# First rows in two loads ahead of U3, and 11 warming transposes in place of 13

## The chip, the cores and the metric
One core of a Trainium2 chip runs the program. The metric is the device time of one execution in microseconds (us), the median of several runs.

## What is computed
A gated graph network over x (64 batches, 128 nodes, 256 features, float32), three steps with one dense adjacency, then a residual and a layer norm:

```python
h = x
for _ in range(3):
    a_in = jnp.einsum('nm,bmd->bnd', adj, h)
    a_out = jnp.einsum('nm,bmd->bnd', adj, h)
    av = jnp.concatenate([a_in, a_out], axis=-1)
    z = sigmoid(av @ w3.T + w3_b + h @ u3.T + u3_b)
    r = sigmoid(av @ w4.T + w4_b + h @ u3.T + u3_b)
    hv = tanh(av @ w5.T + w5_b + (r * h) @ u5.T + u5_b)
    h = (1 - z) * h + z * hv
out = layernorm(x + h)
```

Both aggregates use the same adjacency, so the kernel adds the two halves of w3, w4 and w5 and has one aggregate.

## The kernel before, in words
**Tiling.** The 64 batches are worked on in groups of 4 batches (512 rows); 4 groups make a round, and there are 4 rounds. Within a round each group has three steps, so a round has 12 frames (group and step), interleaved so that TensorE always has a product of one frame to do while the other engines work on another. State is held features first (hT, xT: two chunks of 128 features by 512 rows) for the dense products, and nodes first (hn, x_in) for the aggregate. Every float32 operand of a steady product is split into a high part (ScalarE casts it to fp32r) and a low part (VectorE subtracts), and a product is three matmuls: high weight with low state, low with high, high with high (lines 416 to 420).

**Order.** Each engine has its instruction stream written out by hand and waits on semaphores. SP issues nearly all DMAs; ScalarE issues the first two and the stores. VectorE splits, transposes blocks and updates the state, ScalarE evaluates sigmoid and tanh and makes high parts. GpSimd makes the identity (line 1142) and small constants.

**The start**, which the change touches, has its own code.
- ScalarE issues two loads: `first_in` (line 747), which per partition (node) holds the rows of the first 4 batches (4 x 256 floats) and the transposed adjacency (128 floats), 576 KB; then `lead_in` (line 748), which holds U3 and half 0 of the first group's state, features first, 512 KB. Behind these it loads the activation table (line 751), splits the two halves of the state (line 680), the first aggregate (line 656), W4 and W5 (line 745).
- SP waits for a constant of GpSimd (line 375), then issues half 1 of that state (line 376, 256 KB), W4 (512 KB, line 377 through 373), the biases, W5, W3, the rows of the second group (line 381), and further loads.
- VectorE waits for `lead_in` (line 991), splits U3 (992, 994), makes the low part of state half 0 (line 918), sums the two halves of W4 (line 977), then the low part of state half 1, the low parts of the aggregate (line 865), the low part of W4 (987), the biases (1004), and the sums of W5 and W3.
- TensorE waits for the identity and does 13 transposes of it into a bank that is overwritten later (`keep_warm`, lines 546 to 549), then the first aggregate in full float32 (`first_aggregate`, lines 430 to 441; 2 halves of 2 batches, each batch 2 chunks, 8 matmuls), then the parts of U3 (`first_u`), of W4, of W5 and of W3 (`first_dense`). The aggregate waits for `rows_first` (line 432), the parts of U3 for the splits.

Of the kernel before, what the change touches and what calls it, by code (L numbers as in the profile page):

```python
# [54 lines left out]
P = 128  # L55
EPS = 1e-5


def build(nc, x_rows, first_rows, second_rows, lead, x_cols, w3_t, w4_t, w5_t, u5_t, biases, out_rows):
    N, B, D = out_rows.shape  # L60
    ROWS = 512
    GB = ROWS // N
    C = D // P
    HB = GB // 2
# [7 lines left out]
    DMA = 16  # L72
# [7 lines left out]
    with ctx:  # L80
        def sb(name, shape, dt=F32):
            return ctx.enter_context(nc.sbuf_tensor(name, shape, dt))
# [4 lines left out]
        def sem(name):  # L87
            return ctx.enter_context(nc.semaphore(name))
# [10 lines left out]
        bias = sb("bias", [P, 3, C])  # L99
        wt_hi = [sb(f"wt_hi{k}", [P, C, D], F32R) for k in range(5)]  # L100
        wt_lo = [sb(f"wt_lo{k}", [P, C, D], F32R) for k in range(5)]
        first_in = sb("first_in", [P, GB * D + N])
        adjT = first_in[:, GB * D:GB * D + N]
        W3, W4, W5, U3, U5 = range(5)
        BZ, BR, BV = range(3)

# [16 lines left out]
        aT = sb("aT", [P, QUADS, LINE])  # L123
        z = [sb(f"z{k}", [P, C, ROWS]) for k in range(2)]
        y = [sb(f"y{k}", [P, GB, D]) for k in range(2)]
        x_first = [first_in[:, 0:GB * D].rearrange("p (b d) -> p b d", b=GB), y[1]]
        y_tail = sb("y_tail", [P, GB, D])


# [24 lines left out]
        def by_chunk(bank):  # L154

            return bank.rearrange("p (c r) -> p c r", c=C)
# [24 lines left out]


        x_loaded = [sem(f"x_loaded{k}") for k in range(2)]
        rows_first = sem("rows_first")
        stored = [sem(f"stored{k}") for k in range(2)]


# [15 lines left out]
        rows_second = sem("rows_second")  # L203
# [95 lines left out]
        def _(sp):  # L299
            def load_cols(i, q):  # L300
                sp.dma_start(xT[q][:, :, :], x_cols[bass.ds(SLOTS * i + q, 1), :, :, :]
                             .rearrange("g p c r -> p (g c) r")).then_inc(xT_loaded[q], DMA)
# [69 lines left out]
            def load_wide(k):  # L372
                sp.dma_start(wide[k][:, :, :, :], wide_in[k]).then_inc(w_loaded[k], DMA)
# [4 lines left out]
            sp.dma_start(bias_in[:, :, :], biases).then_inc(bias_loaded, DMA)  # L378
            load_wide(W5)
            load_wide(W3)  # L380
            sp.dma_start(x_first[1][:, :, :], second_rows).then_inc(rows_second, DMA)
            load_cols(0, 1)
            sp.dma_start(square[1][:, :, :], u5_t).then_inc(w_loaded[U5], DMA)
            load_rows(0, 2)
# [30 lines left out]
        def _(pe):  # L415
# [13 lines left out]

            def first_aggregate(j):  # L430

                pe.wait_ge(rows_second if j == 1 else rows_first, DMA)
                for hf in range(2):
                    bank = by_chunk(ps_a[:, hf, :])
                    for bb in range(HB):
                        b = hf * HB + bb
                        for c in range(C):
                            done = nc.tensor.matmul(bank[:, c, bb * N:(bb + 1) * N],  # L438
                                                    x_first[j][:, b, c * P:(c + 1) * P],
                                                    adjT[:, :], start=True, stop=True)  # L440
                    done.then_inc(a_ready, 1)

# [21 lines left out]
            def update_product(i, j, carry):  # L464

                if carry or j >= 2:
                    pe.wait_ge(z_ready, C * frames(*two_before(i, j)))
                u_product(i, j)
# [21 lines left out]
            def second_half(i, j, carry):  # L490

                gate_r(i, j)
                value(i, j, carry)
                if j < FR - 1:
                    gate_z(i, j)

            def candidate(i, j):

                pe.wait_ge(rh_hi_ready, C * frames(i, j))
                pe.wait_ge(rh_lo_ready, C * frames(i, j))  # L500
                for oc in range(C):
                    dense(ps_v, U5, oc, rh_hi, rh_lo, False, True).then_inc(vpre_ready, 1)

            def weight_ready(k):
                pe.wait_ge(wt_hi_ready, PREPARED.index(k) + 1)
                pe.wait_ge(wt_lo_ready, PREPARED.index(k) + 1)
# [6 lines left out]
            def first_u():  # L513

                pe.wait_ge(u3_hi_ready, 1)
                for kc in range(C):
                    pe.wait_ge(hT_hi_ready, kc + 1)
                    for oc in range(C):
                        part(ps_g[0], wt_hi, U3, oc, kc, hT_hi, kc == 0, False)
                    pe.wait_ge(u3_lo_ready, 1)  # L520
                    for oc in range(C):
                        part(ps_g[0], wt_lo, U3, oc, kc, hT_hi, False, False)
                for kc in range(C):
                    pe.wait_ge(hT_lo_ready, kc + 1)
                    for oc in range(C):
                        part(ps_g[0], wt_hi, U3, oc, kc, hT_lo, False, False)

            def first_dense(dst, k, start, stop, done):

                pe.wait_ge(wt_hi_ready, PREPARED.index(k) + 1)  # L530
                pe.wait_ge(a_hi_ready, 2)
                for kc in range(C):
                    for oc in range(C):
                        part(dst, wt_hi, k, oc, kc, aT_hi, start and kc == 0, False)
                pe.wait_ge(a_lo_ready, 2)
                for kc in range(C):
                    for oc in range(C):
                        part(dst, wt_hi, k, oc, kc, aT_lo, False, False)
                pe.wait_ge(wt_lo_ready, PREPARED.index(k) + 1)
                for oc in range(C):  # L540
                    for kc in range(C):
                        end = part(dst, wt_lo, k, oc, kc, aT_hi, False, stop and kc == C - 1)
                    if done:
                        end.then_inc(done, 1)

            def keep_warm(n):

                for _ in range(n):
                    nc.tensor.transpose(ps_g[0][:, 0, 0:P], ident[:, :], ident[:, :])  # L549

            def first_round():

                pe.wait_ge(ident_ready, 1)
                keep_warm(13)
                first_aggregate(0)
                first_u()
                first_dense(ps_g[0], W4, False, True, rpre_ready)
                first_dense(ps_v, W5, True, False, None)
                pe.wait_ge(r_ready, C)
                first_dense(ps_g[0], W3, False, True, zpre_ready)  # L560
                first_aggregate(1)
                update_product(0, 1, False)
                weight_ready(U5)
                candidate(0, 0)
                aggregate(0, 2, first=True)
                for j in range(1, FR - 2):
                    frame(0, j, False)
                second_half(0, FR - 2, False)
# [84 lines left out]
        def _(act):  # L653
# [91 lines left out]
                nc.scalar.copy(wt_hi[k][:, :, :], weight(k)[:, :, :]).then_inc(wt_hi_ready, 1)  # L745

            act.dma_start(first_in[:, :], first_rows).then_inc(rows_first, DMA)
            act.dma_start(lead_in[:, 0:C * D + ROWS], lead).then_inc(lead_loaded, DMA)

            act.wait_ge(neg_half_ready, 1)  # L750
# [19 lines left out]
            j = FR - 1  # L770
# [432 lines left out]
```

## Time and profile before

| | us |
|---|---|
| median of 3 runs | 735.11 (735.06 to 735.43) |
| the profiled execution | 734.97 |
| its span, first to last instruction | 732.9 |
| TensorE busy (page, engines) | 726.1 |
| VectorE busy | 635.7 |
| ScalarE busy | 419.4 |

The span is the time between the first and the last instruction that the profile shows; the profiled execution's own time is 2.1 us more. PE is TensorE's matmuls, PEld its weight loads, which run beside the matmuls, DVE is VectorE, ACT ScalarE, SP SyncE. ACTq and SPq are instructions that issue a DMA. Records of the matmuls overlap, since they are pipelined, so the distance between starts says more than the length of one. A name with an arrow is what is written and what it is written from. In the views by DMA queue q1 is SP's queue and q10 is ScalarE's.

### The profile page before, as it was taken

To read this page: it belongs to the slowest core of one execution; us is meant where nothing else is said; L and a number is where in the kernel's file an instruction comes from. 1 tells how busy PE (TensorE), PEld (TensorE's weight loads), DVE (VectorE), ACT (ScalarE), POOL (GpSimd) and SP (SyncE) were. 2 spreads that over 40 slices of the span, in tenths; PEclk is the share of its full clock that TensorE was granted. 3 is DMA by queue.
4 is the path that set the end of the run, shared out by engine and by line. 5 is a ranking of instruction groups with operands and counts; after the bars stand their busy time and mean duration, and the time that the engine had idled before them with its cause. 6 is when DMAs were issued, how large, how long until landed. Compare 5 with 4: busy or idle time off the path is not lost.

```text
span 732.9 us, 9687 instructions
## 1 busy us (share of the span) xinstructions
PE 726.1 (99%) x3237; PEld 602.3 (82%) x3237; DVE 635.7 (87%) x932; ACT 419.4 (57%) x647; POOL 29.9 (4%) x71
## 2 busy tenths in 40 slices
PE   9999999999999999999999999999999999999997
PEld 7888888888888888888888888888888888888886
DVE  6788898889998888898999888899899987899887
ACT  5645655465666654565566754565556664565546
POOL 0000000000010000000011000000011000000013
PEclk9999999999999999999999999999999999999999
DMA  8145454446766445445567445544467544544442
GB/s 345 61 145 168 136 184 143 140 148 186 237 225 194 160 148 172 152 137 167 188 237 229 156 139 172 184 140 134 163 203 254 195 159 143 164 132 134 142 145 116
DMA packets 74183, 124.13 MB, mean 169 GB/s; under 512 B 8368, under 2 KB 55472, under 8 KB 74160
## 3 DMA queue, kind: packets, MB, share of 16 engines
q1 hardware_dynamic: 72144, 116.43, 48.8%
q10 hardware_dynamic: 2016, 7.41, 2.8%
q8 instruction: 13, 0.21, 0.1%
q14 instruction: 10, 0.08, 0.0%
HBM read 67.18 MB, written 56.62 MB: 169 GB/s over the span
## 4 chain that ended last, share of the span: by engine, by line
PE 98%; DVE 1%; ACT 0%; issue 0%; POOLq 0%; POOL 0%; DVEq 0%
PE ps_g L420 17%; PE ps_g L418 17%; PE ps_g L419 17%; PE ps_v L420 12%; PE ps_v L418 12%; PE ps_v L419 12%; PE ps_a L420 3%; PE ps_a L418 3%; PE ps_a L419 3%; PE ps_g L510 1%; PE ps_a L438 1%; PE ps_g L549 0%; PE ps_v L510 0%; DVE dz L1072 0%; DVE stats L1037 0%
## 5 line engine op out<-in xcount | busy, mean ns | idle before, releaser
L685 ACT ACTIVATE ps_v<-ps_v,bias 128x512 f32<-128x512 f32 x94 | 62.2, 662 | 182.7 <-PE ps_v L420 182.7
L418 PE MATMUL ps_g<-aT_hi,wt_lo 128*128 128x512 f32 (+1 forms) x380 | 147.1, 387 | 0.0
L420 PE MATMUL ps_g<-aT_hi,wt_hi 128*128 128x512 f32 (+1 forms) x380 | 147.0, 387 | 0.0
L419 PE MATMUL ps_g<-aT_lo,wt_hi 128*128 128x512 f32 (+1 forms) x380 | 147.0, 387 | 0.0
L724 ACT ACTIVATE z<-ps_g,bias 128x512 f32<-128x512 f32 x94 | 64.8, 690 | 95.0 <-PE ps_g L420 94.6
L418 PEld LDWEIGHTS ps_g<-aT_hi,wt_lo 128*128 128x128 f32 x380 | 71.3, 188 | 14.6
L419 PEld LDWEIGHTS ps_g<-aT_lo,wt_hi 128*128 128x128 f32 x380 | 71.3, 188 | 14.5
L420 PEld LDWEIGHTS ps_g<-aT_hi,wt_hi 128*128 128x128 f32 x380 | 71.3, 188 | 14.5
L870 DVE TENSOR_TENSOR aT_lo<-aT,aT_hi 128x1024 fp32r<-128x1024 f32 x46 | 56.4, 1225 | 30.4 <-ACT aT_hi L660 30.4
L860 DVE STREAM_TRANSPOSE ab<-ps_a 128x1024 f32<-128x1024 f32 x46 | 57.4, 1249 | 23.5 <-PE ps_a L420 22.3
L418 PE MATMUL ps_v<-rh_hi,wt_lo 128*128 128x512 f32 x192 | 74.7, 389 | 0.0
L419 PE MATMUL ps_v<-rh_lo,wt_hi 128*128 128x512 f32 x192 | 74.7, 389 | 0.0
L420 PE MATMUL ps_v<-rh_hi,wt_hi 128*128 128x512 f32 x192 | 74.7, 389 | 0.0
L708 ACT ACTIVATE r_sb<-ps_g,bias 128x512 f32<-128x512 f32 x94 | 64.9, 690 | 16.3 <-PE ps_g L420 16.3
L418 PE MATMUL ps_v<-aT_hi,wt_lo 128*128 128x512 f32 x188 | 73.2, 389 | 0.0
L418 PE MATMUL ps_g<-hT_hi,wt_lo 128*128 128x512 f32 x188 | 73.2, 389 | 0.0
L419 PE MATMUL ps_g<-hT_lo,wt_hi 128*128 128x512 f32 x188 | 73.1, 389 | 0.0
L419 PE MATMUL ps_v<-aT_lo,wt_hi 128*128 128x512 f32 x188 | 73.1, 389 | 0.0
L420 PE MATMUL ps_g<-hT_hi,wt_hi 128*128 128x512 f32 x188 | 73.1, 389 | 0.0
L420 PE MATMUL ps_v<-aT_hi,wt_hi 128*128 128x512 f32 x188 | 73.1, 389 | 0.0
L892 DVE TENSOR_TENSOR dz<-dz,z 128x512 f32<-128x512 f32 x94 | 64.7, 688 | 1.6
L912 DVE TENSOR_TENSOR rh_lo<-rh,rh_hi 128x512 fp32r<-128x512 f32 x96 | 61.8, 684 | 0.3 <-ACT rh_hi L799 0.2
(126 smaller groups left out, 1237.0 us busy)
## 6 DMA issues: line engine op xcount, KB each, us to landing
turned_a<-ab SPq DMA_DIRECT2D x46, 512.0 KB, 3.7
aT<-turned_a SPq DMA_DIRECT2D x184, 128.0 KB, 3.0
turned_h<-hb SPq DMA_DIRECT2D x46, 512.0 KB, 2.6
hn<-turned_h SPq DMA_DIRECT2D x184, 128.0 KB, 3.0
x_in<-in_x_rows SPq DMA_DIRECT2D x14, 512.0 KB, 4.6
xT<-in_x_cols SPq DMA_DIRECT2D x12, 512.0 KB, 4.3
out<-y ACTq DMA_DIRECT2D x12, 512.0 KB, 3.6
wide<-in_w_t SPq DMA_DIRECT2D x3, 512.0 KB, 6.6
```

What stands on the lines that cost most here:

```text
L418: nc.tensor.matmul(dst, lhs_lo, rhs_hi, start=first, stop=False, skip_group_check=True)
L419: nc.tensor.matmul(dst, lhs_hi, rhs_lo, start=False, stop=False, skip_group_check=True)
L420: return nc.tensor.matmul(dst, lhs_hi, rhs_hi, start=False, stop=last, skip_group_check=True)
L438: done = nc.tensor.matmul(bank[:, c, bb * N:(bb + 1) * N], x_first[j][:, b, c * P:(c + 1) * P], adjT[:, :], start=True, stop=True)
L510: return nc.tensor.matmul(dst[:, oc, :], w[k][:, kc, oc * P:(oc + 1) * P], state[:, kc, :], start=start, stop=stop, skip_group_check=True)
L685: nc.scalar.activation(ps_v[:, oc, :], ps_v[:, oc, :], ACT.Tanh, bias=bias[:, BV, oc:oc + 1]).then_inc(v_ready, 1)
L708: nc.scalar.activation(r_sb[:, oc, :], ps_g[j % 2][:, oc, :], ACT.Sigmoid, bias=bias[:, BR, oc:oc + 1]).then_inc(r_ready, 1)
L724: nc.scalar.activation(z[j % 2][:, oc, :], ps_g[j % 2][:, oc, :], ACT.Sigmoid, bias=bias[:, BZ, oc:oc + 1]).then_inc(z_ready, 1)
L860: nc.vector.transpose(ab[:, :, :].rearrange("p q x -> p (q x)"), ps_a[:, :, :].rearrange("p k x -> p (k x)")).then_inc(ab_ready, 1)
L870: nc.vector.tensor_tensor(quads_first(aT_lo), by_block(aT), f32(quads_first(aT_hi)), ALU.subtract).then_inc(a_lo_ready, 2)
L892: nc.vector.tensor_tensor(dz[:, c, :], dz[:, c, :], z[j % 2][:, c, :], ALU.mult).then_inc(zd_ready, 1)
L912: nc.vector.tensor_tensor(rh_lo[:, c, :], rh[:, c, :], f32(rh_hi[:, c, :]), ALU.subtract).then_inc(rh_lo_ready, 1)
```

## The change
The rows of the first group's first two batches come with the adjacency in one load of 320 KB (`first_in`, now 2 x 256 + 128 floats per partition); the rows of the other two batches come in a second load of 256 KB into the buffer `y[0]`, with a semaphore of its own (`rows_rest`). Both are issued by ScalarE, ahead of `lead_in`, which so becomes the third DMA of that queue. The first aggregate waits for the first load ahead of its first half, and for the second load ahead of its second half. `keep_warm` does 11 transposes in place of 13. Nothing else is changed.

```diff
@@ -56,7 +56,7 @@
 EPS = 1e-5
 
 
-def build(nc, x_rows, first_rows, second_rows, lead, x_cols, w3_t, w4_t, w5_t, u5_t, biases, out_rows):
+def build(nc, x_rows, first_rows, first_rest, second_rows, lead, x_cols, w3_t, w4_t, w5_t, u5_t, biases, out_rows):
     N, B, D = out_rows.shape
     ROWS = 512
     GB = ROWS // N
@@ -99,8 +99,8 @@
         bias = sb("bias", [P, 3, C])
         wt_hi = [sb(f"wt_hi{k}", [P, C, D], F32R) for k in range(5)]
         wt_lo = [sb(f"wt_lo{k}", [P, C, D], F32R) for k in range(5)]
-        first_in = sb("first_in", [P, GB * D + N])
-        adjT = first_in[:, GB * D:GB * D + N]
+        first_in = sb("first_in", [P, HB * D + N])
+        adjT = first_in[:, HB * D:HB * D + N]
         W3, W4, W5, U3, U5 = range(5)
         BZ, BR, BV = range(3)
 
@@ -123,7 +123,11 @@
         aT = sb("aT", [P, QUADS, LINE])
         z = [sb(f"z{k}", [P, C, ROWS]) for k in range(2)]
         y = [sb(f"y{k}", [P, GB, D]) for k in range(2)]
-        x_first = [first_in[:, 0:GB * D].rearrange("p (b d) -> p b d", b=GB), y[1]]
+
+        def x_first(j, b, cols):
+            if j == 0 and b < HB:
+                return first_in[:, b * D + cols.start:b * D + cols.stop]
+            return y[j][:, b, cols]
         y_tail = sb("y_tail", [P, GB, D])
 
 
@@ -181,7 +185,7 @@
 
 
         x_loaded = [sem(f"x_loaded{k}") for k in range(2)]
-        rows_first = sem("rows_first")
+        rows_first, rows_rest = sem("rows_first"), sem("rows_rest")
         stored = [sem(f"stored{k}") for k in range(2)]
 
 
@@ -378,7 +382,7 @@
             sp.dma_start(bias_in[:, :, :], biases).then_inc(bias_loaded, DMA)
             load_wide(W5)
             load_wide(W3)
-            sp.dma_start(x_first[1][:, :, :], second_rows).then_inc(rows_second, DMA)
+            sp.dma_start(y[1][:, :, :], second_rows).then_inc(rows_second, DMA)
             load_cols(0, 1)
             sp.dma_start(square[1][:, :, :], u5_t).then_inc(w_loaded[U5], DMA)
             load_rows(0, 2)
@@ -429,14 +433,17 @@
 
             def first_aggregate(j):
 
-                pe.wait_ge(rows_second if j == 1 else rows_first, DMA)
                 for hf in range(2):
+                    if j == 0:
+                        pe.wait_ge((rows_first, rows_rest)[hf], DMA)
+                    elif hf == 0:
+                        pe.wait_ge(rows_second, DMA)
                     bank = by_chunk(ps_a[:, hf, :])
                     for bb in range(HB):
                         b = hf * HB + bb
                         for c in range(C):
                             done = nc.tensor.matmul(bank[:, c, bb * N:(bb + 1) * N],
-                                                    x_first[j][:, b, c * P:(c + 1) * P],
+                                                    x_first(j, b, slice(c * P, (c + 1) * P)),
                                                     adjT[:, :], start=True, stop=True)
                     done.then_inc(a_ready, 1)
 
@@ -551,7 +558,7 @@
             def first_round():
 
                 pe.wait_ge(ident_ready, 1)
-                keep_warm(13)
+                keep_warm(11)
                 first_aggregate(0)
                 first_u()
                 first_dense(ps_g[0], W4, False, True, rpre_ready)
@@ -745,6 +752,7 @@
                 nc.scalar.copy(wt_hi[k][:, :, :], weight(k)[:, :, :]).then_inc(wt_hi_ready, 1)
 
             act.dma_start(first_in[:, :], first_rows).then_inc(rows_first, DMA)
+            act.dma_start(y[0][:, HB:GB, :], first_rest).then_inc(rows_rest, DMA)
             act.dma_start(lead_in[:, 0:C * D + ROWS], lead).then_inc(lead_loaded, DMA)
 
             act.wait_ge(neg_half_ready, 1)
@@ -1179,7 +1187,8 @@
     bias_names = ("w3", "u3", "w4", "w5", "u5")
     laid = {
         "x_rows": x.reshape(B // GB, GB, N, C, QUADS, BLK).transpose(0, 2, 4, 3, 1, 5).reshape(B // GB, N, GB * D),
-        "first_rows": np.concatenate([x[0:GB].transpose(1, 0, 2).reshape(N, GB * D), adj.T], axis=1),
+        "first_rows": np.concatenate([x[0:GB // 2].transpose(1, 0, 2).reshape(N, GB * D // 2), adj.T], axis=1),
+        "first_rest": x[GB // 2:GB].transpose(1, 0, 2),
         "second_rows": x[GB:2 * GB].transpose(1, 0, 2),
         "lead": np.concatenate([features_first(w("u3"), 1).reshape(P, C * D),
                                 x[0:GB].reshape(GB * N, C, P)[:, 0, :].T], axis=1),
```

## Rows read from the trace of the kernel before

**Rows 1.** The page, busy time of each engine (us, share of the span, instructions)

```profile
PE 726.1 (99%) x3237; PEld 602.3 (82%) x3237; DVE 635.7 (87%) x932; ACT 419.4 (57%) x647; POOL 29.9 (4%) x71
```

**Rows 2.** Windows: stretch, its length, busy (records) of PE, then of DVE

```profile
20.00:715.00 695.00, 695.00 (x3068) 1.00 0.51 166
...
7.80:11.60 3.80, 3.80 (x10) 1.00 1.02 412
```

**Rows 3.** Chain that ended last, in order of time: start, us, what

```profile
1.52 3.03 PE ps_g L549 x13
4.55 2.52 PE ps_a L438 x16
...
716.24 0.87 PE ps_a L597 x8
```

**Rows 4.** Timeline of the start: start, us, instruction, idle time before it and releaser

```profile
5.79 1.28 ACT L680 CAST hT_hi<-lead_in 128x512 fp32r<-128x512 f32 x2 [2.66 <-DMA lead_in<-in_lead]
5.80 0.43 DVE L992 CAST wt_hi<-lead_in 128x512 fp32r<-128x512 f32 x1 [5.80 <-DMA lead_in<-in_lead]
...
7.77 0.69 DVE L977 TENSOR_TENSOR wsum<-wide 128x512 f32<-128x512 f32 x1 [0.21 <-DMA wide<-in_w_t]
...
8.38 0.68 DVE L918 TENSOR_TENSOR hT_lo<-lead_in,hT_hi 128x512 fp32r<-128x512 f32 x1
...
9.11 0.30 PEld L510 LDWEIGHTS ps_g<-hT_lo,wt_hi 128*128 128x128 f32 x2 [0.18 <-DVE hT_lo L918]
...
12.38 0.77 PEld L510 LDWEIGHTS ps_v<-aT_hi,wt_hi 128*128 128x128 f32 x4 [0.22 <-ACT wt_hi L745]
```

**Rows 5.** Windows, PE alone: stretch, length, busy (records), clock, DMA share, GB/s

```profile
3.00:4.00 1.00, 1.00 (x7) 1.00 0.96 376
4.70:5.50 0.80, 0.80 (x4) 1.00 0.87 302
6.00:6.50 0.50, 0.50 (x7) 1.00 0.98 389
```

**Rows 6.** DMA issues of the start: count, KB each, us from issue to landing

```profile
first_in<-in_first_rows ACTq DMA_DIRECT2D x1, 576.0 KB, 3.7
lead_in<-in_lead ACTq DMA_DIRECT2D x1, 512.0 KB, 4.6
...
lead_in<-in_x_cols SPq DMA_DIRECT2D x1, 256.0 KB, 4.9
```

**Rows 7.** Timeline of the start, the instructions that issue DMAs

```profile
0.73 0.40 ACTq L747 DMA_DIRECT2D first_in<-in_first_rows  x1
...
1.16 0.45 ACTq L748 DMA_DIRECT2D lead_in<-in_lead  x1
...
1.55 0.39 SPq L376 DMA_DIRECT2D lead_in<-in_x_cols  x1
...
1.99 0.43 SPq L373 DMA_DIRECT2D wide<-in_w_t  x1
```

**Rows 8.** DMA queues from 0 to 4.6 us, all that moved: packets, MB, share

```profile
q10 hardware_dynamic: 245, 1.00, 61.2%
```

**Rows 9.** Timeline of the steady part, stores beside moves of the state

```profile
367.74 2.02 SPq L325 DMA_DIRECT2D hn<-turned_h  x4
367.81 0.36 ACTq L697 DMA_DIRECT2D out<-y  x1
...
382.77 0.37 ACTq L697 DMA_DIRECT2D out<-y  x1
382.87 2.20 SPq L325 DMA_DIRECT2D hn<-turned_h  x4
```

**Rows 10.** DMA queues, 367 to 369.2 us (one row), then 382 to 385.4 us

```profile
q1 hardware_dynamic: 68, 0.11, 18.8%
...
q10 hardware_dynamic: 119, 0.49, 43.6%
q1 hardware_dynamic: 127, 0.18, 14.6%
```

## The prediction

> **What bounds the kernel now.** I read the page first: TensorE is busy 726.1 of 732.9 us, 99% of the span [rows 1]. Then one long stretch of the view by windows: from 20 to 715 us TensorE is busy in all 695.00 us [rows 2]. So nothing after the start gives way or takes up slack; a shift of the moment at which TensorE gets its work in the first 20 us passes to the end one for one. The change touches only that start, so the rest of the reading is of it.
>
> There TensorE has three pieces of work: 13 warming transposes from 1.52 us, the first aggregate (8 matmuls, which the trace shows as 16 records) from 4.55 us, then the parts of U3 and W4, from about 7.1 us [rows 3]. It seems to be the bound here too, but the other engines' rows show how thin the cover is [rows 4]. VectorE waits for the lead transfer (U3 and half 0 of the state) until 5.80 us, works on it until about 7.56 us, idles 0.21 us until W4's load is in, and sums W4 at 7.77 us. From there it goes on with the low part of the state's half 1 (8.38), the low parts of the aggregate and of W4, the biases and the sum of W5, and is busy in all 3.80 us from 7.8 to 11.6 [rows 2]. Twice this chain stands right before TensorE: the weight load that belongs to hT_lo's half 1 waited 0.18 us and started at 9.11, after VectorE's end at 8.38 + 0.68 = 9.06; the first load of W5 waited 0.22 us for ScalarE's split of W5 and started at 12.38. The loads run about 0.2 us ahead of their matmuls, so these waits cost TensorE next to nothing now, but they leave no room either: **the start has two paths of equal length**, TensorE's own and the one from W4's landing over VectorE.
>
> **The clock.** The profile shows a granted clock of 1.00 in each stretch [rows 5], but the spacing says that TensorE ran at half of it at first: 13 transposes took 3.03 us, 0.23 each [rows 3], where eight of the same shape took 0.87 us, 0.11 each, at the end [rows 3]. TensorE worked on 4 records in the 0.8 us from 4.7 to 5.5 and on 7 in the 0.5 us from 6.0 to 6.5 [rows 5]: the rise from 1.2 to 2.4 GHz lies between, and it had worked without a break since 1.52 us.
>
> **The parts.** (a) Two transposes less: 2 × 3.03/13 = 0.47 us of TensorE time. They end at 1.52 + 11 × 0.233 = 4.08 us in place of 4.55.
>
> (b) The rows and the adjacency. The first load goes from 576 to 320 KB. It was issued at 0.73 us and landed 3.7 us later, at 4.43 [rows 6]. 256 KB less at 376 GB/s (the rate from 3 to 4 us [rows 5]) is 0.70 us: it lands at about 3.75, before 4.08. The second load (256 KB) brings the sum to the old 576 KB, so it lands at about 4.45 to 4.6. It is wanted after half of the aggregate, 8 of 16 records, at the slow spacing 8 × 0.23 = 1.8 us later, at 5.9. Neither wait costs anything; should one come late, the path over VectorE still covers it by some 0.4 us.
>
> (c) One more issue on ScalarE. Each takes 0.40 to 0.45 us [rows 7], so the lead's issue moves from 1.16 to about 1.60, and what is queued behind it on ScalarE, the load of the activation table and the probe, by as much. After these ScalarE waits for the lead anyway, 2.66 us now [rows 4]. The issue time by itself is hidden too, since the queue is still moving rows then. What isn't hidden is the **order**. SyncE issues half 1 of the state (256 KB) at 1.55 us, and W4 at 1.99 [rows 7]. Before, the lead was 0.39 us ahead of that, and until 4.6 us only the ACT queue (q10) moved data, 245 packets, none of SP's [rows 8], though SP's transfer had been issued 3 us before. Now SP's half 1 (1.55) is issued just ahead of the lead (1.60).
>
> How such near ties go, two places in the steady part show [rows 9, 10]. SP at 367.74 and ACT at 367.81: until 369.2 only SP's queue (q1) moved data, and ACT's came behind its first transfer. ACT at 382.77 and SP at 382.87: by 385.4 both had moved about equally many packets, 119 and 127. So SP's transfer goes ahead or they alternate. In the first case the lead is later by the whole 256 KB; in the second too, since half 1 has 128 packets like the lead and is through before the lead is. The price of these 256 KB stands in the rows: half 1 landed at 1.55 + 4.9 = 6.45 us, the lead at 1.16 + 4.6 = 5.76 [rows 6, 7], 0.69 us apart. The bounds are 0 (the ACT queue goes first all the same) and 0.87 (256 KB at the 302 GB/s of 4.7 to 5.5 us [rows 5]). I take 0.69.
>
> The Trainium skill (DMA: Bandwidth & Descriptors, Queues, rings and completion order) says that each DMA engine takes packets from the queue rows with work in turn. The rows at 382 us agree, the start before doesn't: there one queue was emptied first. By the page's rule the lead would be delayed by half 1 whatever the order of issue, so the same 0.69 us; by the order of issue it is the same again.
>
> (d) Smaller packets. The rows came in 128 packets of 4.6 KB, now in 128 of 2.5 KB and 128 of 2 KB. Where 2 KB packets (half 1 of the state) made up most of the traffic, from 4.7 to 5.5 us, the rate was 302 GB/s, against 376 from 3 to 4 us with the large ones [rows 5]. 576 KB at 340 in place of 376 GB/s is 0.17 us more. Bounds: 0, and 0.39 us (all 576 KB at 302). I take 0.15. It delays the lead, W4 and all behind them.
>
> **The sum.** The lead lands 0.69 + 0.15 = 0.84 us later, at 6.60 in place of 5.76. VectorE's idle 0.21 us takes the first part; the rest, 0.63 us, moves W4's sum from 7.77 to 8.40 (W4's own load, in at 7.77 + 0.15 = 7.92, no longer decides). Since VectorE then works without a gap up to W5, hT_lo's half 1 and W5 come 0.63 us later. TensorE, through with the aggregate near 6.6, waits until ScalarE has split half 0 (6.60 + 0.64 = 7.24 us), then again for hT_lo's half 1 (9.69) and, if anything is left, for W5 (12.96). The 0.47 us from (a) are gone in the first of these waits, the loads' lead of up to 0.2 us takes a little off. I forecast **+0.6 us**. Against the profiled execution's own 734.97 (span 732.9 and 2.1 around it) that is 735.57; the median of the runs, 735.11, is 0.14 above it: 735.7.
>
> A measurement of this kernel can tell 0.2%, 1.47 us, from no change; this is 0.08%.
>
> **The rivals.**
> A, *the lead keeps its place* (the ACT queue goes first as in the start now; for it: SP's transfer, long issued, moved nothing at first [rows 8]; against it: the two near ties [rows 9, 10]). The lead is late by 0.15 alone, at 5.91, VectorE's 0.21 us cover that, W4 is late by 0.15, and so is W5. The two transposes are hidden behind VectorE. 735.11 + 0.15 = 735.3. That the rows in fact land no sooner belongs here, as TensorE only waits earlier for the same end.
> B, *the transposes pay*: W4 lands sooner, or the order of transfers gives VectorE its work sooner, so that TensorE's 0.47 us count. For it: TensorE is what the chain of waits names throughout. Against it: no byte ahead of W4 is taken away, and the two weight loads that waited [rows 4]. 735.11 − 0.4 = 734.7.
> C, *the other side, clearly slower*: W4's 512 KB get ahead of the lead as well. W4 is issued at 1.99, while the lead's issue would run from 1.60 to 2.05. Then the lead lands with W4's time now, about 7.77 + 0.15 = 7.92, which is 2.12 later than 5.80; less 0.21 that is +1.9 us, 737.0. It passes 0.2% from a lead that lands 1.7 us later, at 7.4. For it: W4's issue starts before the lead's ends. Against it: 0.39 us between the starts of two issues kept their order whole [rows 7, 8].
> D, *the clock rises later*, since a transposes' stretch is shorter. Each us of delay costs half a us, and 0.5 of it would be hidden; against it: TensorE works on without a break past 5.7 us. It has no more than 3 in 100.
>
> **Chances.** The forecast 0.52, A 0.30, B 0.09, C 0.06, D 0.03. The range takes in B (734.7) and the forecast with both upper bounds, 0.87 + 0.39 − 0.21 = 1.05 us, 736.2; C and D stay outside. Faster by over 0.2% would need 1.47 us, three times what the transposes hold: 0.01. Slower by over 0.2%: C and a part of D, 0.06. Within: 0.93.
>
> **What would show it.** In the profile after: SP's half 1 lands before the lead; lead near 6.6, ScalarE's and VectorE's first work there; W4's sum at 8.4 with no idle time ahead of it; the aggregate from 4.1 us; TensorE idle some 0.6 us ahead of the first U3 part, and W5's first part near 13.0 in place of 12.42. If the lead lands by 6.0, A is right; if W4's sum starts before 7.77, B; if the lead lands past 7.4, C. TensorE idle between 20 and 715 us would break the first premise, that shifts pass on whole.

## Result: slower by 0.6%, and where it went

| | kernel before | changed kernel |
|---|---|---|
| median | 735.17 us (735.06 to 735.66, 6 runs) | 739.47 us (738.85 to 741.57, 6 runs) |
| ratio, 95% interval | | 1.0059 (1.0048 to 1.0069) |
| the profiled execution | 734.97 us | 741.57 us |
| its span | 732.9 us | 739.5 us |
| mean granted clock | 1.000 | 0.997 |
| lead's first use on VectorE | 5.80 us | 9.54 us |

The changed kernel is 4.3 us slower in the median and also spreads more, 2.7 us between its runs where the kernel before has 0.6. Its profiled execution is the slowest of the six, 6.6 us above that of before. So the account below is of an unusually slow execution; what varies from run to run is taken up with the experiments.

The chain that ended last of the changed kernel, in order of time (start, us, what):

```profile
1.65 7.87 DMA lead_in<-in_lead
9.52 0.02 issue
9.54 0.63 ACT hT_hi L687
10.17 0.14 issue
10.30 7.35 PE ps_g L517 x24
17.66 2.72 PE ps_v L517 x12
```

and further on in the same view, over the whole span:

```profile
718.49 1.32 issue
719.81 0.50 PE ps_g L422
```

These rows hold nearly the whole loss. The chain of the kernel before began with TensorE [rows 3]; here it goes through the lead load. The parts of U3 start at 10.30 in place of about 7.1 us, 3.2 us later. The 24 matmuls behind take 7.35 us where they took 5.5 before: 1.8 us for a clock that falls. And at 718.49 TensorE stands for 1.32 us and waits for nothing that the profile shows. (This standing still while nothing is waited for is called the stand below.) That makes 3.2 + 1.8 + 1.3 = 6.3 of 6.6 us; the last 0.3 us are not placed.

**The lead.** The timeline of the changed kernel beside [rows 4, 7]:

```profile
0.74 0.40 ACTq L754 DMA_DIRECT2D first_in<-in_first_rows  x1
1.17 0.45 ACTq L755 DMA_DIRECT2D y<-in_first_rest  x1
...
1.55 0.39 SPq L380 DMA_DIRECT2D lead_in<-in_x_cols  x1
1.65 0.45 ACTq L756 DMA_DIRECT2D lead_in<-in_lead  x1
1.99 0.43 SPq L377 DMA_DIRECT2D wide<-in_w_t  x1
...
3.91 1.78 PEld L445 LDWEIGHTS ps_a<-first_in 128*128 128x128 f32 x8 [0.17 <-DMA first_in<-in_first_rows]
...
9.54 1.14 ACT L687 CAST hT_hi<-lead_in 128x512 fp32r<-128x512 f32 x2 [5.91 <-DMA lead_in<-in_lead]
9.54 0.43 DVE L1000 CAST wt_hi<-lead_in 128x512 fp32r<-128x512 f32 x1 [9.54 <-DMA lead_in<-in_lead]
...
10.27 0.30 PEld L517 LDWEIGHTS ps_g<-hT_hi,wt_hi 128*128 128x128 f32 x2 [2.88 <-DVE wt_hi L1000]
```

The issues stand where the prediction put them, and the aggregate starts early, at 3.9 us. But the lead comes 3.7 us later than before, where 0.84 had been forecast, and TensorE has no work from 7.6 to 10.3 us. The queues of the changed kernel from 7 to 9.2 us (packets, MB, share) tell how little was missing by then:

```profile
q1 hardware_dynamic: 345, 0.77, 92.5%
q10 hardware_dynamic: 10, 0.03, 3.7%
```

The lead is 128 packets of 4 KB. In these 2.2 us 10 packets of ScalarE's queue moved, among 345 of SyncE's. Spread over 16 DMA engines, 8 for each, 10 is what one or two engines hold (worked out, the view doesn't name engines). The packet records of the trace, which no view lists one by one, agree: the last five 4 KB packets of ScalarE's queue ended at 7.76, 8.07, 8.38, 8.69 and 9.00 us. Each took 0.16 us and they are 0.31 us apart, which leaves room for just one 4 KB packet of another load between two of them, as one DMA engine would show that serves the two queues in turn. Half 1 of the state was in at 1.55 + 6.3 = 7.85 us, so from then on the other load is W4 or one behind it. The lead was used at 9.54 us, after the last of these packets: it has landed when its slowest engine is through.

**The clock.** Windows of the changed kernel, PE alone (stretch, length, busy, clock, DMA share, GB/s):

```profile
2.00:3.00 1.00, 1.00 (x7) 1.00 0.88 268
3.00:4.00 1.00, 1.00 (x7) 1.00 0.91 301
4.00:5.00 1.00, 1.00 (x6) 1.00 0.84 270
...
7.60:10.30 2.70, 0.09 (x1) 1.00 0.99 387
11.00:12.00 1.00, 1.00 (x5) 0.55 1.02 418
12.00:13.00 1.00, 1.00 (x4) 0.50 1.01 412
13.00:14.00 1.00, 1.00 (x3) 0.50 1.06 424
14.00:15.00 1.00, 1.00 (x5) 0.75 1.03 412
```

TensorE did next to nothing from 7.6 to 10.3 us. Its clock was still granted in full when work came back, and fell to half only after 11 us, in the midst of work, until about 14.5 us. The matmuls' starts agree: two of them fill 0.55 us at first (10.30 to 10.85) and 0.85 us later (11.51 to 12.36).

At the start, the rise from 1.2 to 2.4 GHz was late as well. The first aggregate's records in the changed kernel, and below them in e11_w4_after_landing, one of the experiments, with the same 11 transposes and the same start at 3.9 us:

```profile
3.93 2.06 PE L445 MATMUL ps_a<-first_in 128*128 128x128 f32 x8
5.77 1.91 PE L445 MATMUL ps_a<-first_in,y 128*128 128x128 f32 x8
```

```profile
3.92 1.31 PE L446 MATMUL ps_a<-first_in 128*128 128x128 f32 x8
5.07 1.06 PE L446 MATMUL ps_a<-first_in,y 128*128 128x128 f32 x8
```

In the changed kernel all 16 records have the slow spacing of 0.23 us (5.77 - 3.93 for 8), and the aggregate ends at about 7.7 us; in e11 the rise came right behind the transposes and it ends at about 6.1. The moment of the rise differs as much with 13 transposes: 2.1 us from the aggregate's start to its end in e1_warm13, 3.5 us in e5_bias_second. Here it cost nothing, as the lead was later still.

The GB/s column answers a second question. The same windows of the kernel before:

```profile
2.00:3.00 1.00, 1.00 (x6) 1.00 0.92 313
3.00:4.00 1.00, 1.00 (x7) 1.00 0.96 376
4.00:5.00 1.00, 1.00 (x5) 1.00 1.03 393
```

313 + 376 + 393 = 1082 KB in 3 us against 268 + 301 + 270 = 839 KB: by 5 us the changed kernel is 0.24 MB behind, which at 376 GB/s is 0.65 us. What of this is the smaller packets is open, as e5_bias_second below shows.

**The stand at 718 us.** TensorE's weight loads in the changed kernel's timeline there:

```profile
717.88 0.19 PEld L424 LDWEIGHTS ps_g<-hT_hi,wt_hi 128*128 128x128 f32 x1
719.81 0.19 PEld L422 LDWEIGHTS ps_g<-aT_hi,wt_lo 128*128 128x128 f32 x1 [1.74 <-issue]
```

The same two instructions follow each other without a gap in the kernel before (712.90 and 713.13 us). What moved over the DMA queues from 717 to 719.8 us is one packet:

```profile
q8 instruction: 1, 0.02, 2.6%
```

It is a load of instructions, under way just before the stand, at 717.3 us. The kernel before has such packets too: 11 in its first 300 us, none from 300 to 709, one at 709.2 and one at 714.8, and no stand.

### The profile page after: what moved, and what is told of

The parts are those of the page before. It is cut to its first block, busy times and chain, and to the rows that moved or that the text cites. A ratio compares the mean times of both kernels' runs of the same rounds, so it can differ in the third digit from the quotient of the medians.

```text
span 739.5 us, 9684 instructions
## 1 busy us (share of the span) xinstructions
PE 728.8 (99%) x3235; PEld 604.4 (82%) x3235; DVE 635.8 (86%) x932; ACT 419.4 (57%) x647; POOL 29.6 (4%) x71
## 4 chain that ended last, share of the span: by engine, by line
PE 97%; DMA 1%; DVE 1%; issue 0%; ACT 0%; ACTq 0%; POOLq 0%; POOL 0%; DVEq 0%
PE ps_g L422 17%; PE ps_g L423 17%; PE ps_g L424 17%; PE ps_v L424 12%; PE ps_v L423 12%; PE ps_v L422 12%; PE ps_a L424 3%; PE ps_a L423 3%; PE ps_a L422 3%; PE ps_g L517 1%; DMA lead_in<-in_lead 1%; PE ps_v L517 0%; PE ps_a L445 0%; DVE dz L1080 0%; DVE stats L1045 0%
## 5 line engine op out<-in xcount | busy, mean ns | idle before, releaser
L423 PEld LDWEIGHTS ps_g<-aT_lo,wt_hi 128*128 128x128 f32 x380 | 71.4, 188 | 14.5
L424 PEld LDWEIGHTS ps_g<-aT_hi,wt_hi 128*128 128x128 f32 x380 | 71.4, 188 | 14.5
```

The source lines that it names most:

```text
L423: nc.tensor.matmul(dst, lhs_hi, rhs_lo, start=False, stop=False, skip_group_check=True)
L424: return nc.tensor.matmul(dst, lhs_hi, rhs_hi, start=False, stop=last, skip_group_check=True)
```

## The experiments

Three causes were to be told apart: the place of the lead among the loads (called Order, later Share), the split into more and smaller packets or the third load on the queue as such (Split, Third), and the two transposes less (Warming by the clock, Fetch by where the instructions lie, Timing by the shifted start). Each kernel was timed in rounds beside the kernel before.

### e1_warm13: 13 transposes again

```diff
-                keep_warm(11)
+                keep_warm(13)
```

> The changed kernel with 13 warming transposes again. Theory Order (the lead load lands late because it is now issued among SyncE's loads, and TensorE stands still until it is there): nothing changes, since the transposes end far ahead of 9.5 us: lead near 9.5 us, 739 to 740 us. Rival Warming (fewer transposes let the clock fall): the clock keeps its level after 10 us and the time falls by the 1.7 us that 3.4 us at half the clock cost, to about 737.5 or below.

737.12 us (736.51 to 740.23), ratio 1.0026 (1.0015 to 1.0037): 2.3 us faster than the changed kernel, or 1.2 us by the latter's second timing below, which neither theory said. Its profile, of the slowest of its eight runs, has the lead at 9.85 us, TensorE idle for 4.1 us and the fall of the clock, just as the changed kernel has; Order holds for these. Warming falls, since the clock falls with 13 too. What is gone is the stand at 718 us, of which neither theory had thought.

### e2_warm11: the kernel before with 11

```diff
-                keep_warm(13)
+                keep_warm(11)
```

> The kernel before with 11 transposes, one load for all rows. Theory Order: the lead load keeps its place and lands at 5.8 us, so the time stays within 0.3 us of before, 735.0 to 735.5; TensorE waits for the rows from 4.08 to 4.5 us. Rival Warming: slower by over 1 us, and a granted clock below 1.00 somewhere in the first 15 us.

736.91 us (736.46 to 737.6), ratio 1.0023 (1.0014 to 1.0033). The lead is at 5.95 us, the granted clock 1.00 throughout the first 20 us, and yet it is 1.5 us slower: both expectations miss. Two of TensorE's idle times in it are:

```profile
PE ps_g L418 <- issue: 1.0, 1, 1.0
PE ps_a L438 <- DMA first_in<-in_first_rows: 0.4, 1, 0.4
```

The second row is the wait for the rows, as expected. The first is the stand again, near 715 us. So taking two transposes out costs about 1 us at the far end of the run, with no part in the loads. The rest of the 1.9 us between the two profiles' spans is mostly at the start, in the chain that ended last:

```profile
4.54 3.20 PE ps_a L438 x16
7.74 5.46 PE ps_g L510 x24
```

The aggregate took 3.20 us in place of 2.52 [rows 3], as the clock rose later, and the parts of U3 start 0.66 us later.

### e8_tiny, e14_warm13_tiny: is it the work or the instructions?

```diff
-                keep_warm(13)
+                keep_warm(11)
+                tiny()
```

with `tiny` one 32 by 32 float32 matmul of the identity, two weight loads and two matmuls on TensorE, as many instructions as the two transposes have.

> The kernel before with 11 transposes and one tiny matmul (32 by 32) behind them, which is as many TensorE instructions as the two transposes taken out (2 weight loads, 2 matmuls) and next to no work. It asks where the 1.5 us of the same kernel without the tiny matmul came from. Theory Fetch (the stand of 1.0 us near 715 us, at a point where TensorE waits for nothing and a 16 KB instruction load is under way, depends on where the instructions lie): the stand is gone and 0.2 to 0.6 us are left from the start, 735.4 to 736.0. Rival Timing (the stand comes from the shifted time or from less warming): it stays and the time is 736.7 to 737.1.

735.48 us (735.14 to 736.16), ratio 1.0002 (0.9992 to 1.0011), and no stand. 1.4 us are back though the work of two transposes stays out. What theory Fetch said came true and what Timing said didn't: with the count of instructions as before, the stand is gone.

> The kernel before with all 13 transposes and the tiny matmul besides, so that the instructions behind it lie 4 further on where 11 transposes alone put them 4 back. The work adds at most 0.4 us. If the stand goes by where the instructions lie relative to what the last load brought, a shift forward either leaves it hidden (735.3 to 735.9, no stand) or brings a stand of over 1 us at another place. If it goes by the work, or by TensorE's first 5 us, there is none.

Edit: all 13 transposes and `tiny()` behind them. 735.28 us (735.11 to 735.84), ratio 1.0000 (0.9991 to 1.0009), no stand. This leaves the question where it was: a shift forward by 4 instructions is harmless, one back by 4 isn't, which Fetch allows but this run alone doesn't show. The evidence for it is e8_tiny, and a count over all 16 profiles: the 7 of kernels with 11 transposes and nothing in their place have a stand of 1.0 to 1.6 us at that point, the 9 others have none. The packet records add to it. An instruction packet starts ahead of the weight load with which TensorE goes on: by 2.3 to 2.9 us in the seven profiles with a stand (712.71 and 715.09 us in e2), by 3.4 to 5.3 us in the nine without (709.19 and 713.13 us in the kernel before). So the packet comes later, measured against the work, where there is a stand. That the stand is TensorE waiting for these instructions fits all of this, but no view names it, and why four instructions less move the packet so far isn't shown.

### e3_lead_second, e5_bias_second: who is third?

e3 is the changed kernel with the lead issued second:

```diff
             act.dma_start(first_in[:, :], first_rows).then_inc(rows_first, DMA)
-            act.dma_start(y[0][:, HB:GB, :], first_rest).then_inc(rows_rest, DMA)
             act.dma_start(lead_in[:, 0:C * D + ROWS], lead).then_inc(lead_loaded, DMA)
+            act.dma_start(y[0][:, HB:GB, :], first_rest).then_inc(rows_rest, DMA)
```

> The changed kernel with the lead load issued second and the rest of the rows third. Theory Order: the lead lands near 5.3 us (320 KB ahead of it in place of 576), and now the rest of the rows, issued at 1.65 us, is what gets mixed with SyncE's loads: it lands at 6.5 to 8 us where it is wanted at 5.8, so 735 to 737.5 us. Rival Split (the split into more and smaller packets, or a third load on ScalarE's queue, slows the queue as a whole): the lead still lands 1 us or more later than the 5.8 us of before and the time stays at 738 or above.

740.31 us (739.61 to 741.08), ratio 1.007 (1.0053 to 1.0087). The landings are what Order said: lead used at 5.20 us, the rest of the rows at 7.70. The time isn't, by 2.8 us; in its profile are a wait of 2.3 us for these rows, the fall of the clock, and the stand of 1.1 us:

```profile
PE ps_a L445 <- DMA y<-in_first_rest: 2.3, 1, 2.3
...
PE ps_g L422 <- issue: 1.1, 1, 1.1
```

The fall of the clock and the stand had no place in the expectation. In e5 the kernel before keeps its one load of all rows and 13 transposes; only the 5 KB of the biases are moved:

```diff
+            act.dma_start(bias_in[:, :, :], biases).then_inc(bias_loaded, DMA)
             act.dma_start(lead_in[:, 0:C * D + ROWS], lead).then_inc(lead_loaded, DMA)
...
-            sp.dma_start(bias_in[:, :, :], biases).then_inc(bias_loaded, DMA)
```

> The kernel before (13 transposes, all rows in one load), but the 5 KB load of the biases moved from SyncE to ScalarE, between the rows and the lead. So the lead is again the third load, issued at about 1.65 us, while no row load is split and the large bytes are the same. Theory Order: the lead lands at 8 us or later and the time is 737.5 to 740. Rival Split: the lead lands by 6.1 us, within 0.5 us of before, 735.0 to 735.7.

739.33 us (737.73 to 740.26), ratio 1.0047 (1.0032 to 1.0061). The lead is used at 8.98 us. **The loss at the start is made here with no row load split**, by a lead that is issued at 1.65 in place of 1.16 us behind another load. Split falls as the cause of it. The rate falls here too: 300, 303 and 178 GB/s from 2 to 5 us, 781 KB with the rows in large packets, less than the changed kernel's 839 (e3, with the rows split and the lead second, has 970). Small packets of the rows thus aren't all that made the changed kernel's loads slow.

### e4_sp_after_lead, e7_w4_after_lead, e10_sp_after_rows, e11_w4_after_landing: what overtakes the lead?

e4, a semaphore that ScalarE sets once it has issued the lead, ahead of all of SyncE's loads; e7, the same ahead of W4 alone:

```diff
+            act.sem_inc(lead_issued, 1)
...
-            sp.wait_ge(neg_half_ready, 1)
+            sp.wait_ge(lead_issued, 1)
```

> The changed kernel, but SyncE issues its first load only after ScalarE has issued all three (at about 2.1 us in place of 1.55). Theory Order: ScalarE's queue is emptied first, the lead lands at 5.8 to 6.1 us, W4's sum starts at 7.8 to 8.1, the clock stays at 1.00, 735.0 to 735.6 us. Rival Split: the lead lands at 8 us or later, 738 or above.

738.88 us (738.64 to 739.91), ratio 1.005 (1.0034 to 1.0067): the expectation misses. SyncE's first issue is at 2.17 us, 0.5 us behind the lead's, and still the lead is used at 8.53 us. From 7 to 9.2 us the queues moved

```profile
q1 hardware_dynamic: 376, 0.85, 100.0%
q10 hardware_dynamic: 9, 0.02, 2.8%
```

that is, again a few packets of the lead among hundreds of SyncE's. The order of issue doesn't protect a load. The neighbour is another one here: half 1 was in at 2.17 + 6.5 = 8.67 us only, after the lead, and ScalarE's last four packets (0.16 us each) ended at 7.39, 7.59, 7.82 and 8.06 us, the later ones 0.24 us apart: room for one 2 KB packet of half 1 (0.08 us) between two of them.

> The changed kernel, but SyncE issues W4 (512 KB) only after the lead has been issued; half 1 of the state (256 KB) keeps its near tie with the lead. The forecast on record charged the lead with these 256 KB alone: then the lead lands at 6.4 to 6.8 us and the time is 735.5 to 736. W4 is issued 0.4 us after the lead already in the changed kernel, so if W4 is not what overtakes, the lead stays at 9 us or later and the time at 739.

738.17 us (737.8 to 740.54), ratio 1.0048 (1.0029 to 1.0066); the lead is used at 7.45 us. W4's issue moved by 0.2 us only (2.17), and the lead lies between both cases of the expectation. With its stand of 1.3 us taken off, its span of 735.9 us is 1.7 above that of before.

e10 lets SyncE start only when the first rows have landed (with `tiny()`, so without the stand):

```diff
-            sp.wait_ge(neg_half_ready, 1)
+            sp.wait_ge(rows_first, DMA)
```

> The changed kernel with the tiny matmul, and SyncE issues its first load only when the first rows have landed (about 3.9 us). Its data can then move from about 4.9 us, when ScalarE's three loads are nearly through. Theory Share (the lead is late because its packets share the DMA engines with SyncE's loads, on some of the 16 engines for long): the lead lands at 5.6 to 6.2 us, W4 at 7.9 to 8.5, the time is 735.3 to 736. Rival Third (a third load on a queue is served late whoever competes): the lead at 7.3 us or later, 737 or more.

735.81 us (735.69 to 736.25, 10 runs), ratio 1.0005 (0.9996 to 1.0015). Share holds: this is the changed kernel with its split, its three loads in one queue and its 11 transposes, no longer told apart from the kernel before. It is 2.5 to 3.7 us faster than the changed kernel's two medians (738.28 and 739.47), but 1 us or more of that is what `tiny()` takes away. Against the same kernel without the new wait (e9, 736.51 us on the same chip, and e13, 737.23, both below) the wait gains 0.7 to 1.4 us, and the runs lie within 0.6 us where those of e9 spread over 2.8. The timeline:

```profile
3.67 0.39 SPq L380 DMA_DIRECT2D lead_in<-in_x_cols  x1
...
6.50 0.43 DVE L1005 CAST wt_hi<-lead_in 128x512 fp32r<-128x512 f32 x1 [6.50 <-DMA lead_in<-in_lead]
...
8.76 0.69 DVE L990 TENSOR_TENSOR wsum<-wide 128x512 f32<-128x512 f32 x1 [0.50 <-DMA wide<-in_w_t]
```

The lead is a little outside what was expected, 6.50 in place of at most 6.2. SyncE's data moved from about 5 us, when most of the lead was through. The windows have 268, 315 and 320 GB/s from 2 to 5 us, 0.18 MB less than before, which at 376 GB/s is 0.5 us. That would be most of the 0.7 us against 5.80. Whether that is packet size, the one load more or SyncE's packets beside the lead's end (89 of SyncE's and 54 of ScalarE's from 5 to 6.2 us) isn't told apart; the kernel before's own loads had the lead in use at 5.80, 5.83 (e14), 5.95 (e2) and 6.71 us (e8) in four profiles.

e11 waits with W4 and all behind it for the lead's landing:

```diff
+            sp.wait_ge(lead_loaded, DMA)
             load_wide(W4)
```

> The changed kernel, but SyncE issues W4 and all behind it only when the lead has landed; half 1 of the state (256 KB) still competes with the lead. It measures the term of the forecast, half 1 alone ahead of the lead. By the forecast the lead lands at 6.4 to 6.7 us. If half 1 alone can hold back single engines for long: 7.3 us or later. The time itself grows, since W4 is issued near 6.6 and lands near 8.9 to 9.2: W4's sum 1.2 to 1.5 us later than before, and with the stand near 718 us 737.6 to 738.2.

The lead is used at 7.29 us, outside the 6.4 to 6.7 of the forecast and at the edge of what would speak against it. Against the 6.50 of e10, half 1 costs 0.8 us, close to the 0.69 of the forecast; these are one profile each, and e10's lead wasn't quite alone. The rest is what e10 lost against the kernel before. No packet of ScalarE's queue moved after 7 us here, and the four runs lie within 0.7 us of each other. With W4 in flight, in the seven profiles that have the changed kernel's loads (its own two, e1, e6, e9, e13, and e7 with W4 0.2 us later), the lead was used at 7.25 to 9.85 us. So **the tail, where these seven have one, goes with W4**; four of them had next to none, so the one profile of e11 could be without it by luck. The small spread of its runs (0.7 us against 2.6 to 3.7 in the two timings each of the changed kernel and of it with `tiny()`, and in e1) and the 4 KB gaps between the lead's last packets speak against luck. The time, 739.46 us (739.2 to 739.85), ratio 1.0055 (1.0038 to 1.0072), is over 1 us more than expected: W4's sum came at 11.11 us, 3.3 us later than before, since a load issued anew at 7 us takes 3.8 us.

### e6_fill_gap: what the clock costs

```diff
                 first_aggregate(0)
+                keep_warm(26)
                 first_u()
```

> The changed kernel with 26 more transposes between the first aggregate and the first part of U3, where TensorE stood still from 7.6 to 10.3 us. It tells what of the loss is the late load and what the fall of the clock after it. If the fall is caused by the standstill: granted clock 1.00 throughout, 1.7 us less in the profile than the changed kernel, 737 to 738 us, with a smaller spread. If it isn't: 739 to 740 and the dip stays.

737.93 us (736.82 to 738.16), ratio 1.0032 (1.002 to 1.0043). The clock keeps 1.00; in its chain the U3 parts start as late as in the changed kernel and take 5.48 us:

```profile
7.45 2.84 PE ps_g L556 x26
10.29 5.48 PE ps_g L517 x24
```

Against 7.35 us that is the 1.8 us of the clock. Each of the four profiles with a fall (the changed kernel's, e1, e3, e5) has TensorE idle for 1.9 us or more before it, so a standstill seems to be needed. It isn't enough, and no fixed length of it decides: in e4 TensorE was idle for 3.0 us and the clock stayed, in e5 1.9 us were followed by a fall. The rows of e4:

```profile
6.30:9.30 3.00, 0.01 (x1) 1.00 0.92 351
9.30:11.00 1.70, 1.70 (x7) 1.00 1.03 419
11.00:12.00 1.00, 1.00 (x6) 1.00 1.00 410
```

and of e5, one ending at 9.7 us with a fall past 10:

```profile
7.80:9.70 1.90, 0.02 (x1) 1.00 1.03 415
10.00:11.00 1.00, 1.00 (x5) 0.89 1.04 426
11.00:12.00 1.00, 1.00 (x3) 0.50 1.01 414
```

The 26 transposes also hold back TensorE where the lead comes sooner (7.36 us in this profile), so the time is no measure of the clock alone. The Trainium skill (TensorE: Matmul & The Clock Gate, Part 4: PE-mode transpose) says that transposes don't count as work for the clock in the way matmuls do. With 26 of them as all that TensorE did from 7.45 to 10.29 us it stayed at 2.4 GHz, and in none of the seven runs was the mean clock below 0.998. That speaks against the rule without settling it, since e4's clock outlasted 3.0 us of nothing. The start of e11 says more: there the clock rose when TensorE had done next to nothing but its 11 transposes, 8 records of the aggregate taking 1.15 us from the start (3.92 to 5.07) where the slow spacing needs 1.84.

### e9_after_tiny, e12_after_again, e13_tiny_again: how much is the stand?

The changed kernel with `tiny()` behind its 11 transposes (e9), then the changed kernel itself and e9 again on one chip.

> The changed kernel with the same tiny matmul behind its 11 transposes. Theory Fetch: the stand of 1.3 us near 718 us is gone, the late lead stays, so 737.2 to 738.5. Rival Timing: 739 to 740.

736.51 us (735.99 to 738.83), ratio 1.002 (1.001 to 1.0029), no stand, lead at 8.50 us. The 3.0 us below the changed kernel were more than a stand can hold, and the two had been timed on different chips.

> The changed kernel unaltered, on one chip with the next. If the two seen causes make up the loss (late lead by 1.3 to 3.8 us, stand of 1.0 to 1.7 us, and 1.7 us more where the clock falls), the median lies 1.0 to 1.7 us above the next run's: 737.5 to 739. If something else is in it, the distance is 2.5 us or more, as between the two chips.

> The changed kernel with the tiny matmul behind its 11 transposes, as before: 736.3 to 737.5, no stand near 718 us, lead between 7.3 and 9.5 us.

The changed kernel took 738.28 us (737.39 to 740.66), the one with `tiny()` 737.23 us (736.1 to 738.7), ratios 1.0047 (1.0031 to 1.0063) and 1.0031 (1.0019 to 1.0042). On one chip the distance is 1.05 us, as the stand alone would have it. Their profiles match in the start (lead at 7.47 and 7.25 us) and differ in span by 2.1 us, 736.2 and 734.1. TensorE's idle times in the first, beside the wait for the identity that every profile has,

```profile
PE ps_g L422 <- issue: 1.6, 1, 1.6
...
PE ps_g L517 <- ACT hT_hi L687: 0.8, 1, 0.8
```

and in the second:

```profile
PE ps_g L517 <- ACT hT_hi L692: 0.9, 1, 0.9
```

So the stand is 1.0 to 1.6 us in each of the seven profiles that have it, and the start is the rest, which changes from one execution to the next with the lead. (The intervals of the two ratios overlap; it is the profiles that tell the two kernels apart.)

## Why the prediction was wrong

It forecast 735.7 us, within 0.2%, and gave slower by more a chance of 0.06. By its own steps:

1. *"So nothing after the start gives way or takes up slack; a shift ... passes to the end one for one."* The second half held: a late start came out late at the end. But it was read as if nothing after the start could change. Two transposes are also four instructions, and their removal brought a stand of 1.0 to 1.6 us near 718 us. This step alone is 0.14 to 0.22%. No row of the trace of before shows it; the instruction loads have their own queue in the page, the last two of them at 709 and 715 us, and that a place in the run could hang on them wasn't asked.
2. *Part (a), the transposes*: the aggregate starts at 3.9 us, near the 4.08 forecast, and brings nothing, since TensorE has to wait for the lead. That TensorE would be "through with the aggregate near 6.6" was wrong by 1.1 us (about 7.7), as the clock rose later; with the lead where it was forecast, TensorE would have been the later of the two. **(b)** held: the rows landed at 0.74 + 3.1 = 3.84 and 1.17 + 3.4 = 4.57 us, no wait for the second.
3. *Part (c), the order*: that the lead would get SyncE's half 1 ahead of it was right, and the price was near, 0.8 us (e11 less e10, one profile each) for 0.69, where half 1 is all that competes. What failed is that W4 was left to rival C, "W4's 512 KB get ahead of the lead as well", with 0.06. W4 needn't get ahead as a whole. As the packet times have it, it shares single DMA engines with the last packets of the lead, and the landing is that of the slowest one: 0 to 2.6 us more than the 7.29 of e11. "0.39 us between the starts of two issues kept their order whole" was read from a kernel where the lead was second; e4, with 0.5 us, refutes it for a third load. The rule of the Trainium skill cited there (DMA: Bandwidth & Descriptors, Queues, rings and completion order), that an engine takes packets from the queue rows in turn, agrees with this tail (one packet per 0.31 us) better than the order of issue does; it was held to change nothing because only half 1 was put into it.
4. *Part (d), smaller packets*: 0.15 us taken with an upper bound of 0.39. e10, where little else competes, has the lead 0.7 us later and 0.5 us of data less by 5 us. The bound came from a rate with 2 KB packets in a mix, 302 GB/s, against 376; the windows of the changed kernel have 268, 301 and 270. But e5 lost as much rate with large packets, so the term for the loads together was too small, and what packet size has of it stays open.
5. *Rival D, the clock*: it thought of a late rise, which came (and cost 0.66 us in e2, none here), not of a fall. The forecast itself had TensorE idle for 0.6 us; it never asked what a longer standstill does. 1.8 us in executions where it falls.

The sum for the profiled execution, against the forecast's 735.57: TensorE's work on U3 starts 3.2 us later than before, of which the forecast had 0.6 in its total, so 2.6 us; the clock 1.8; the stand 1.3; that is 5.7 of the 6.0 us to 741.57.

What stays open is why a load issued third on its queue, ahead of SyncE's by 0.5 us, has packets behind SyncE's on some engines, while one issued second has none to speak of. No run issues the lead second but 0.5 us later, so its place and its moment aren't told apart. Both the kernel before and e8_tiny have the lead second; in e8_tiny's profile it was used at 6.71 us, so a small tail can come there too.

## What to carry to other kernels

A load that the first work hangs on should have nothing issued beside it that isn't needed sooner: it lands with its slowest DMA engine, and one more load ahead of it, even of 5 KB, can put a large neighbour's packets among its last ones; holding back the neighbour by 2 us (e10, 3.67 in place of 1.55 us) cost nothing that could be measured against the kernel before. Read the DMA queues in the last stretch before a landing, not only the landing. And when instructions are taken out ahead of a long stretch of work, look over the whole new timeline for a stand that waits for nothing; putting the same count of instructions back tells in one run whether it is theirs. No version here beats the kernel before.

## What was not expected of the hardware

- Taking 4 TensorE instructions out of the first microseconds made a stand of 1.0 to 1.6 us near 715 us, next to a 16 KB instruction load; 4 tiny ones in their place removed it (736.91 to 735.48 us). Where the stand is, that load starts 2.3 to 2.9 us ahead of TensorE's next instruction, elsewhere 3.4 us or more.
- The clock fell 0.6 to 1.1 us after TensorE had gone back to work, not during the standstill (10.3 and 11.1 us in the changed kernel), and a standstill of 1.9 us was followed by a fall while one of 3.0 us wasn't.
- Moving 5 KB from one queue to the other ahead of a 512 KB load made that load 3.2 us later in its profile (5.80 to 8.98 us).
- The lead's last packets moved one per 0.31 us, twice their own 0.16 us, while SyncE's queue had hundreds under way.
